# Five edits joined, and the first layer's gradient summed with X and taken through the keys' weight once

## The chip, the cores and the metric

The kernel runs on one core of a Trainium2 chip. A core has TensorE (PE, matmuls into PSUM), VectorE (DVE), ScalarE (ACT), GpSimd (POOL) and SyncE (SP, which only issues transfers here); the compute engines run their own instruction streams and meet at semaphores. The metric is the device time of one execution in microseconds.

## The reference, cut

Four layers follow each other on 4 x 1024 tokens of width 256: gated linear attention, a mixture of 8 experts (2 per token) and a shared one, a test-time memory, and an MLP with ternary weights. Each is added to its input and normalized. The change touches the first and the third. Of the third:

```python
keys = x @ Wk + bk
queries = x @ Wq + bq
values = x @ Wv + bv
alr = MAX_ALR * jax.nn.sigmoid(x @ Wlr + blr).reshape(-1)
def loss_fn(ps):
    pred = _lmm(ps, kf)          # two layers h = h + silu(h @ W + b)
    per_tok = jnp.mean((pred - vf) ** 2, axis=-1)
    return jnp.sum(per_tok * alr)
grads = jax.grad(loss_fn)(params)
new_params = ...                 # p * (1 - LR * WD) - LR * g / (|g| + EPS)
retrieved = _lmm(new_params, queries)
```

The gradient of W1 is keys^T dz1 over all tokens. Since keys = X Wk + bk, it is also Wk^T (X^T dz1) + bk^T (sum of dz1 over the tokens).
Of the first layer: S = gate * S + k v^T per token, y = q S, with 16 heads of 16 and q, k = elu + 1 of projections.

## The kernel before

The kernel is a sequence of blocks of instructions, one stream per engine, with a barrier between blocks. The order inside a stream is the order of the code; no scheduler is involved.

**Attention** (`build_attention`) works on 32 tiles of 128 tokens, tile j being batch j % 4, chunk j // 4. The loop is skewed: step n runs from -5 to 32, and in it each engine takes the scores of tile n + 1, the attention of tile n and the output of n - 1. ScalarE's `project` makes relu(-x), relu(x) and exp of one of four projections (Q = 0 to 3: queries, queries, keys, keys of chunk 0), and `phi` adds two of them, on VectorE for chunk 0 and on GpSimd later. The gates (a sigmoid, 16 heads in each group of 32 rows) go to memory (`gates_out`, four DMAs), and come back spread over all partitions (`gates_in`, 1 MB a tile). `decay(j)` is one scan of 2048 elements on VectorE over them; it gives the decay between all pairs of a tile's tokens. `weigh(j)` multiplies the scores with it, `weigh_k` the transposed keys. SP's queue is the order of all loads: X^T of chunk 0, weights, gates out, gates of tiles 0 and 1, X^T of chunk 1, Wo, and so on.

**Experts** (`build_expert_tiles`): a loop over 71 tiles of gathered rows; its results go to memory (`outs`). Then an own block (`clear_released`, on GpSimd alone) clears semaphores.

**Memory layer** (`build_memory`): 8 blocks of 512 tokens. Before its blocks TensorE zeroes two PSUM banks gW that hold the gradients, and makes the shared expert's last 512 tokens (L1391, L1396). VectorE combines gathered rows (`combine`), takes moments (`scales`), ScalarE normalizes. All other PSUM banks are a ring of three pairs that the uses of a block take in turn (`pair`, 11 uses a block), so a use waits for the reader of the third use before it. TensorE's order in a block q is: second(q), grad1(q-1), turn_h0(q), turn_x(q+1), turn_h1(q), keys, targets, rates of q+1, back(q), turn_dz2(q), first(q+1), grad2(q), turn_dz1(q). `turn_*` are eight transposes each whose results ScalarE copies to the token-major tiles t_h0, t_h1, t_dz2, t_dz1, which are operands of `grad` (L1361). `rates` multiplies X^T with the column Wlr repeated 128 times, so that all 128 partitions hold the same 512 rates; ScalarE's sigmoid makes alr (L1480), and VectorE multiplies with it in `second` (L1638). After block 7 come the last gradient, five `queries` in between, AdamW on VectorE of the biases, W2 and W1 (five operations each), and a barrier. **Read and MLP** (`build_read_and_mlp`) is not touched.

The init semaphore counts VectorE's memsets (1 to 4: ones, zb, bsum, magic) and the two operations that make lr_w (5, 6), which wait for the weights. These lines say who waits there:

```python
pe.wait_ge(init, 6)
for k in range(2):
    pe.matmul(gW[k][:, :], zb[:, 0:P], zb[:, :], start=True, stop=False, skip_group_check=True)
...
v.wait_ge(w_in, 16 * 6)
v.wait_ge(init, 4)
for g in range(G):
    v.tensor_scalar(lr_w[:, g, :], ones[:, :], Wlr[:, g:g + 1], None, ALU.mult).then_inc(init, 1)
```

## Time and profile before

| | |
|---|---|
| median of 3 runs | 1439.4 us (1431.15, 1439.4, 1440.06) |
| the profiled execution | 1432.35 us, span 1430.6 us |
| PE busy in the span | 1333.4 us (93%), 7684 instructions |
| DVE busy | 797.2 us (56%) |
| ACT busy | 577.5 us (40%) |
| POOL busy | 303.3 us (21%) |
| attention | 0 to about 290 us |
| shared expert and routes | to 446 us |
| experts | to 877 us |
| memory layer | 878 to 1193 us |
| read and MLP | 1193 to the end |

TensorE's share is an average over stages. The attention stage has its own limit, the others theirs, and each stage begins when the one before has ended. So each part of the change is read at its own place in the timeline. Times in the rows are from the span's start; "x16" behind a row is the number of instructions merged in it; idle time and its releaser stand in brackets.

### The profile page before, as it was taken

What the parts mean: (1) busy time and instruction counts of PE and PEld (TensorE: products, weight loads), DVE (VectorE), ACT (ScalarE), POOL (GpSimd) and SP (SyncE); (2) the same over time, 40 slices, a digit from 0 to 9 for tenths busy, and PEclk for the clock granted to TensorE, in tenths of its full rate; (3) what the DMA queues carried; (4) which work ended last, traced back from release to release, by engine and by line L of the source; (5) the groups of instructions that cost most, each with busy time, mean ns of one, the idle gap of its engine ahead of it and who ended that gap; (6) DMA issues with size and microseconds to landing.
All of it is one profiled execution on the core that took longest, in us unless ns stands there. A gap on an engine that the chain in (4) does not pass through costs nothing. (4 is left out here: it accounts for less than half of the span.)

```text
span 1430.6 us, 22465 instructions
## 1 busy us (share of the span) xinstructions
PE 1333.4 (93%) x7684; PEld 847.5 (59%) x7685; DVE 797.2 (56%) x1543; ACT 577.5 (40%) x1271; POOL 303.3 (21%) x345
## 2 busy tenths in 40 slices
PE   7999999899998999999999997789999998899995
PEld 4556666655545666666666664345655564577774
DVE  5999999965331222222222221467778656676764
ACT  5577777541101222222222221234444433566665
POOL 2133333314750000000000003522220000244353
PEclk9999999999999999999999998999999999999999
DMA  5665565574220111111111113212110000000001
GB/s 203 207 199 205 206 210 204 198 266 168 99 82 8 37 44 48 47 44 44 44 44 44 48 48 100 78 30 88 30 30 0 1 0 12 1 1 16 30 16 60
DMA packets 76741, 115.83 MB, mean 81 GB/s; under 512 B 10032, under 2 KB 62576, under 8 KB 72560
## 3 DMA queue, kind: packets, MB, share of 16 engines
q1 hardware_dynamic: 70096, 97.89, 20.3%
q0 software_dynamic: 6144, 16.79, 3.6%
q8 instruction: 52, 0.85, 0.2%
q14 instruction: 33, 0.27, 0.1%
q10 hardware_dynamic: 416, 0.03, 0.0%
HBM read 82.86 MB, written 31.82 MB: 80 GB/s over the span
## 5 line engine op out<-in xcount | busy, mean ns | idle before, releaser
L1759 POOL DMA_INDIRECT m_got<-outs,slot x64 | 61.2, 956 | 566.0 <-DMA outs<-XT 453.9
L1164 DVE TENSOR_TENSOR ro_h<-ro_bB,ro_sl 128x512 f32<-128x512 f32 x71 | 49.1, 692 | 217.3 <-PE ro_bB L1113 217.3
L588 DVE TENSOR_TENSOR_SCAN a_dcy<-a_gbc,a_ident 128x2048 f32<-128x2048 f32 x32 | 142.5, 4453 | 6.0 <-DMA a_gbc<-gd 2.2
L2115 POOL TENSOR_TENSOR q_hr<-q_hf,q_hr 128x512 fp32r<-128x512 f32 x64 | 83.9, 1320 | 283.3 <-ACT q_hr L1956 283.3
L1108 PE MATMUL ro_bA<-Win,ro_xT 128*128 x284 | 134.6, 596 | 0.8 <-ACT ro_xT L1135 0.6
L1120 PE MATMUL ro_bO<-Wout,ro_hT 128*128 x568 | 134.3, 379 | 0.9 <-DVE ro_hT L1157 0.9
L1120 PEld LDWEIGHTS ro_bO<-Wout,ro_hT 128*128 128x128 f32 x568 | 107.8, 190 | 45.6 <-issue 34.6
L1113 PE MATMUL ro_bB<-Wsw,ro_xT 128*128 x284 | 133.4, 592 | 0.0
L1144 ACT ACTIVATE XT<-ro_bO 128x256 f32<-128x256 f32 x71 | 27.2, 383 | 204.9 <-PE ro_bO L1120 204.9
L1157 DVE COPY ro_hT<-ro_bH 128x512 f32<-128x512 f32 x71 | 49.1, 691 | 101.2 <-PE ro_bH L1093 101.2
L1113 PEld LDWEIGHTS ro_bB<-Wsw,ro_xT 128*128 128x128 f32 x284 | 54.0, 190 | 67.9 <-issue 67.9
L1881 PE MATMUL q_bO<-W2r,q_hr 128*128 128x256 f32 x512 | 75.8, 293 | 6.8 <-POOL q_hr L2115 6.7
L1139 ACT ACTIVATE ro_sl<-ro_bA 128x512 f32<-128x512 f32 x71 | 42.4, 597 | 96.1 <-PE ro_bA L1108 96.1
L1881 PEld LDWEIGHTS q_bO<-W2r,q_hr 128*128 128x128 f32 x512 | 66.1, 188 | 19.9 <-POOL q_hr L2115 14.2
L597 DVE TENSOR_TENSOR a_A<-a_bS,a_dcy 128x1024 f32<-128x1024 f32 x64 | 75.0, 1212 | 2.3 <-PE a_bS L335 2.3
L1009 POOL DMA_INDIRECT rows<-r_row,r_rix x64 | 63.3, 989 | 61.2 <-DVE r_rix L910 42.1
L676 POOL TENSOR_TENSOR a_qk<-a_eb,a_rb 128x512 f32<-128x512 f32 x28 | 40.0, 1430 | 164.0 <-ACT a_eb L442 164.0
L1871 PE MATMUL q_bH<-q_xr,W1r 128*128 128x512 f32 x256 | 70.7, 404 | 3.6 <-ACT q_hr L1956 3.6
L1108 PEld LDWEIGHTS ro_bA<-Win,ro_xT 128*128 128x128 f32 x284 | 48.3, 190 | 35.5 <-issue 35.2
L1189 PE MATMUL m_ring<-m_h,m_W 128*128 128x512 f32 x128 | 59.9, 612 | 10.0 <-ACT m_alr L1480 6.4
L861 ACT ACTIVATE sh_sl<-sh_bA 128x512 f32<-128x512 f32 x28 | 16.6, 596 | 122.1 <-PE sh_bA L791 67.9
L1955 ACT ACTIVATE q_hf<-q_bH,q_b 128x512 f32<-128x512 f32 x64 | 44.2, 690 | 37.6 <-PE q_bH L1871 36.4
(281 smaller groups left out, 2506.6 us busy)
## 6 DMA issues: line engine op xcount, KB each, us to landing
a_gbc<-gd SPq DMA_DIRECT2D x32, 1024.0 KB, 5.5
rows<-a_zero SPq DMA_DIRECT2D x8, 1152.0 KB, 9.2
XT<-rows SPq DMA_DIRECT2D x71, 128.0 KB, 2.0
outs<-XT SPq DMA_DIRECT2D x71, 128.0 KB, 1.7
a_xt<-in_xTt SPq DMA_DIRECT2D x8, 512.0 KB, 5.8
X<-in_x SPq DMA_DIRECT2D x8, 512.0 KB, 3.9
Win<-in_w_in SPq DMA_DIRECT2D x8, 512.0 KB, 9.8
Wsw<-in_w_sw SPq DMA_DIRECT2D x8, 512.0 KB, 9.8
```

What stands on the lines that cost most here:

```text
L588: v.tensor_tensor_scan(dcy[:, :], gbc[j % 2][:, :], ident16[:, :], 0.0, ALU.mult, ALU.add).then_inc(d_done, 1)
L597: v.tensor_tensor(A[j % 2][:, 2 * h:2 * h + 2, :, :, :].rearrange("p r g e t -> p r g (e t)"), bS[:, 2 * h:2 * h + 2, :].rearrange("p r (g ...
L1009: pool.indirect_dma_start(out=mem["rows"], out_offset=bass.IndirectOffsetOnAxis(ap=rix[p][k][:, 0:1], axis=0), in_=row[p][k][:, :], in_off ...
L1108: mm = pe.matmul(bA[:, :], xT[p][:, g, :], w, start=(g == 0), stop=(g == G - 1))
L1113: mm = pe.matmul(bB[:, :], xT[p][:, g, :], w, start=(g == 0), stop=(g == G - 1))
L1120: mm = pe.matmul(bO[:, 0:D], hT[:, j * P:(j + 1) * P], Wout[:, bass.ds(e, 1), j, :].rearrange("p o f -> p (o f)"), start=(j == 0), stop=(j ...
L1157: v.tensor_copy(hT[:, :], bH[:, :]).then_inc(ht_read, 1)
L1189: mm = pe.matmul(banks[o][:, :], W[:, i, col + o * P:col + (o + 1) * P], rhs(i), start=(i == 0), stop=(i == G - 1))
L1759: pool.indirect_dma_start(out=got[q % 2][k][:, t, :], out_offset=None, in_=mem["outs"], in_offset=bass.IndirectOffsetOnAxis(ap=slot[:, k, ...
L1871: mm = pe.matmul(bH[f % 2][:, :], W1r[:, g, f * P:(f + 1) * P], xr[q % 2][:, part, g, :], start=(g == 0 and part == 0), stop=(g == G - 1 a ...
L1881: mm = pe.matmul(bO[k // 2][:, (k % 2) * D:(k % 2 + 1) * D], hr[:, part, f % 4, k * P:(k + 1) * P], W2r[:, f, :], start=(f == 0 and part = ...
L2115: pool.tensor_tensor(hr[:, 1, f % 4, :], hf[f % 2][:, :], hr[:, 0, f % 4, :], ALU.subtract).then_inc(hl_done, 1)
```

## The change

In attention: `gates_out` and `decays_out` are one DMA each for all 128 rows instead of four, the memory tensors being padded to 32 rows a batch. X^T of chunk 1 is loaded ahead of the first gates. Tile 0's gates come in two halves, and its scan is two scans (`first_decay`), the first behind phi(1), the second behind phi(3). For the keys of chunk 0 ScalarE leaves the relu(x) out, and VectorE takes it from PSUM in one operation with the addition. TensorE has a hand-written step -1.

Between experts and memory layer: the semaphores are cleared by GpSimd inside the experts' block, and an own block for it is gone.

In the memory layer: TensorE's zeroing matmuls wait for 2 memsets instead of 6; ScalarE loads the sigmoid's table before the first normalize; the rates are made for four groups of 128 tokens in 32 columns each, so that 4 rows of a 128 x 128 tile hold all 512, and these go to memory and come back spread over the partitions (two DMAs on SP's queue a block, `spread_rates`); VectorE waits for that load (`al_in`) and no longer for ScalarE. The gradient of W1 is summed as X^T dz1, with the token-major X that is there; turn_h0 and its copies go, and the ring has 10 uses. Behind the last block ScalarE copies the sum (gx), and TensorE takes it through Wk and adds bk times the sums of dz1 (`through_keys`), which `row_of_sums` has turned into a row.

The core of the diff, attention and then the rest:

```diff
-                    for b in range(B):
-                        sp.dma_start(mem["gd"][T, b], gT[T % 2][32 * b:32 * b + H, :]).then_inc(gd_out, 16)
+                    sp.dma_start(mem["gd"][T].rearrange("b h t -> (b h) t"), gT[T % 2][:, :]).then_inc(gd_out, 16)
...
+                        sp.dma_start(gbc[0][:, h * 8 * P:(h + 1) * 8 * P],
+                                     mem["gd"][0, 0, 8 * h:8 * h + 8].rearrange("h t -> (h t)").rearrange("(o n) -> o n", o=1).to_broadcast([P, 8 * P])).then_inc(g0_in[h], 16)
+
+                load_x(1)
                 gates_out(0)
-                gates_in(0)
+                first_gates_in()
                 gates_in(1)
-                load_x(1)
...
+                    if n == -1:
+                        gates(1)
+                        project(4)
+                        turn_k(0)
+                        scores(0)
+                        values(0)
+                        continue
...
-                    act.activation(rb[Q % 2][:, :], projected(Q), ACT.Relu, scale=s).then_inc(qk_read, 1)
+                    if Q != 2 and Q != 3:
+                        act.activation(rb[Q % 2][:, :], projected(Q), ACT.Relu, scale=s).then_inc(qk_read, 1)
                     act.wait_ge(n_done, Q + 1)
-                    act.activation(eb[Q % 2][:, :], nb[:, :], ACT.Exp, scale=-1.0).then_inc(qk_read, 1)
+                    act.activation(eb[Q % 2][:, :], nb[:, :], ACT.Exp, scale=-1.0).then_inc(qk_read, 2 if Q == 2 or Q == 3 else 1)
...
-                    v.tensor_tensor(qk[0][:, Q // 2, Q % 2, :], eb[Q % 2][:, :], rb[Q % 2][:, :], ALU.add).then_inc(phi_done, 1)
+                    if Q < 2:
+                        v.tensor_tensor(qk[0][:, 0, Q, :], eb[Q][:, :], rb[Q][:, :], ALU.add).then_inc(phi_done, 1)
+                    else:
+                        v.scalar_tensor_tensor(out=qk[0][:, 1, Q % 2, :], in0=projected(Q), scalar=0.0, in1=eb[Q % 2][:, :],
+                                               op0=ALU.max, op1=ALU.add).then_inc(phi_done, 1)
...
+                def first_decay(h):
+                    v.wait_ge(g0_in[h], 16)
+                    v.wait_ge(id_done, 1)
+                    c = slice(h * 8 * P, (h + 1) * 8 * P)
+                    v.tensor_tensor_scan(dcy[:, c], gbc[0][:, c], ident16[:, c], 0.0, ALU.mult, ALU.add).then_inc(d_done if h else d0_done, 1)
...
-                    if Q == 1:
-                        decay(0)
+                    if Q == 1 or Q == 3:
+                        first_decay(Q // 2)
```

```diff
+                def spread_rates(q):
+                    sp.wait_ge(lr_read, q + 1)
+                    sp.dma_start(mem["ad"][q], al4[0:P:32, :]).then_inc(al_out, 16)
+                    sp.wait_ge(al_out, 16 * (q + 1))
+                    if q >= 1:
+                        sp.wait_ge(dp_done, 2 * q)
+                    sp.dma_start(alr[:, :], mem["ad"][q].rearrange("k t -> (k t)").rearrange("(o n) -> o n", o=1).to_broadcast([P, 512])).then_inc(al_in, 16)
+
+                for q in range(3):
+                    spread_rates(q)
                 sp.wait_ge(k_read, 2 * 3)
...
                 def keys(q):
                     if q >= 1:
-                        pe.wait_ge(th0_read, 2 * q)
+                        pe.wait_ge(sl2_done, 2 * q)
...
-                    for g in range(G):
-                        mm = pe.matmul(b[0][:, :], lr_w[:, g, :], tokens(q)(g), start=(g == 0), stop=(g == G - 1))
+                    for k in range(4):
+                        for g in range(G):
+                            mm = pe.matmul(b[0][32 * k:32 * k + 32, 0:P], lr_w[:, g, :], XT[:, g, q * 512 + k * P:q * 512 + (k + 1) * P],
+                                           start=(g == 0), stop=(g == G - 1))
...
                 def grad1(q):
-                    pe.wait_ge(th0_read, 2 * (q + 1))
                     pe.wait_ge(td1_read, 2 * (q + 1))
-                    grad(0, "h0", "dz1").then_inc(g1_ready, 1)
+                    grad(0, X[:, 4 * q:4 * q + 4, :], "dz1").then_inc(gx_ready, 1)
+
+                def row_of_sums():
+                    b = pair(NB, Z2)[0]
+                    pe.wait_ge(bsum_done, NB)
+                    for g in range(G):
+                        mm = pe.matmul(b[0:1, g * P:(g + 1) * P], bsum[:, g:g + 1], ident[:, :], start=True, stop=True)
+                    mm.then_inc(sr_ready, 1)
+
+                def through_keys():
+                    pe.wait_ge(gx_read, 1)
+                    pe.wait_ge(sr_read, 1)
+                    pe.wait_ge(bk_in, 16)
+                    for i in range(G):
+                        for j in range(G):
+                            pe.matmul(gW[0][:, i * D:(i + 1) * D], Wk[:, j, i * P:(i + 1) * P], gx[:, j * D:(j + 1) * D], start=(j == 0), stop=False)
+                        mm = pe.matmul(gW[0][:, i * D:(i + 1) * D], bk_row[:, i * P:(i + 1) * P], s_row[:, :], start=False, stop=True)
+                    mm.then_inc(g1_ready, 1)
...
-                pe.wait_ge(init, 6)
+                pe.wait_ge(init, 2)
...
                     second(q)
                     if q >= 1:
                         grad1(q - 1)
-                    turn_h0(q)
                     turn_x(q + 1)
                     turn_h1(q)
...
+                pe.wait_ge(td2_read, 2 * NB)
+                row_of_sums()
                 grad1(q)
...
+                pe.wait_ge(sr_read, 1)
                 queries(3, pair(q + 1, Z2))
+                through_keys()
                 pe.wait_ge(q_read, 2 * 3)
-                queries(4, pair(q + 1, TH0))
+                queries(4, pair(q + 1, TX))
...
-                    act.activation(alr[:, :], pair(q - 1, LR)[0][:, :], ACT.Sigmoid, bias=blr[:, 0:1]).then_inc(lr_read, 1)
+                        act.wait_ge(al_out, 16 * q)
+                    act.activation(al4[:, :], pair(q - 1, LR)[0][:, 0:P], ACT.Sigmoid, bias=blr[:, 0:1]).then_inc(lr_read, 1)
 
...
+                act.wait_ge(init, 4)
+                act.activation(junk[:, :], ones[:, 0:1], ACT.Sigmoid)
                 normalize(0)
...
+                act.wait_ge(sr_ready, 1)
+                act.activation(s_row[:, :], pair(NB, Z2)[0][0:1, 0:D], ACT.Copy).then_inc(sr_read, 1)
+                act.wait_ge(gx_ready, NB)
+                act.activation(gx[:, :], gW[0][:, :], ACT.Copy).then_inc(gx_read, 1)
...
-                    v.wait_ge(lr_read, q + 1)
+                    v.wait_ge(al_in, 16 * (q + 1))
...
-        build_expert_tiles(nc, mem, "ro_", NI, shared=False)
+        build_expert_tiles(nc, mem, "ro_", NI, shared=False, after={"pool": lambda pool: clear_released(nc, pool)})
         experts.close()
-        clear_released(nc)
```

TensorE in attention around step -1, before and then of the change (bS are scores or projections of chunk 0, bQ a projection, bV the values, bK the transposed keys, bY the gates):

```order
L258 MATMUL a_bS<-a_xt0,a_Wqk 128x512 x8
L335 MATMUL a_bS<-a_qm0,a_qk0 128x256 x8
L267 MATMUL a_bY<-a_xt1,a_WgT 32x128 x8
L258 MATMUL a_bQ<-a_xt1,a_Wqk 128x512 x2
L280 MATMUL a_bV<-a_Wv,a_xt0 128x256 x2
L384 MATMUL a_bK<-ident,a_qk0 128x128 x2
L335 MATMUL a_bS<-a_qm1,a_qk0 128x256 x8
```

```order
L263 MATMUL a_bS<-a_xt0,a_Wqk 128x512 x8
L272 MATMUL a_bY<-a_xt1,a_WgT 32x128 x8
L263 MATMUL a_bQ<-a_xt1,a_Wqk 128x512 x2
L389 MATMUL a_bK<-ident,a_qk0 128x128 x2
L340 MATMUL a_bS<-a_qm0,a_qk0 128x256 x8
L285 MATMUL a_bV<-a_Wv,a_xt0 128x256 x2
L340 MATMUL a_bS<-a_qm1,a_qk0 128x256 x8
```

The gates and projection of chunk 1 and the keys' transposes have moved ahead of the first scores, and the values behind them.

VectorE in attention up to the second scan, before and then of the change (a_qk<- is phi, a_dcy<-a_gbc a scan, a_A the weighing, a_kw the weighing of the keys):

```order
L575 MEMSET a_gT 128x1
L579 TENSOR_TENSOR a_qk<-a_eb,a_rb 128x512 x2
L588 SCALAR_TENSOR_TENSOR a_dcy<-a_gbc,a_ident 128x2048
L579 TENSOR_TENSOR a_qk<-a_eb,a_rb 128x512 x2
L597 TENSOR_TENSOR a_A<-a_bS,a_dcy 128x1024 x2
L605 TENSOR_TENSOR a_kw<-a_bK,a_dcy 128x256
L588 SCALAR_TENSOR_TENSOR a_dcy<-a_gbc,a_ident 128x2048
```

```order
L588 MEMSET a_gT 128x1
L593 TENSOR_TENSOR a_qk<-a_eb,a_rb 128x512 x2
L608 SCALAR_TENSOR_TENSOR a_dcy<-a_gbc,a_ident 128x1024
L595 SCALAR_TENSOR_TENSOR a_qk<-a_bS,a_eb 128x512 x2
L608 SCALAR_TENSOR_TENSOR a_dcy<-a_gbc,a_ident 128x1024
L619 TENSOR_TENSOR a_A<-a_bS,a_dcy 128x1024 x2
L627 TENSOR_TENSOR a_kw<-a_bK,a_dcy 128x256
L602 SCALAR_TENSOR_TENSOR a_dcy<-a_gbc,a_ident 128x2048
```

The scan of 2048 in front of two phi has become one of 1024 ahead of them and one behind; these two phi read PSUM.

TensorE in the memory layer, block 1 from second(1) to back(1), before and then of the change (m_ring is the ring of PSUM pairs, m_gW the gradients; the turns of X are written bank by bank in the middle):

```order
L1361 MATMUL m_gW1<-m_t_dz1,m_t_h0 128x256 x8
L1336 MATMUL m_ring00<-ident,m_h0 128x128 x4
L1336 MATMUL m_ring01<-ident,m_h0 128x128 x4
L1292 MATMUL m_ring10<-ident,X 128x128
...
L1336 MATMUL m_ring20<-ident,m_h1 128x128 x4
L1336 MATMUL m_ring21<-ident,m_h1 128x128 x4
L1189 MATMUL m_ring00<-XT,m_Wk 128x512 x2
...
L1311 MATMUL m_ring20<-XT,m_lr_w 128x512 x2
L1189 MATMUL m_ring00<-m_dz2,m_W2T 128x512 x2
```

```order
L1400 MATMUL m_gW1<-m_t_dz1,X 128x256 x8
L1332 MATMUL m_ring20<-ident,X 128x128
L1332 MATMUL m_ring21<-ident,X 128x128
...
L1378 MATMUL m_ring00<-ident,m_h1 128x128 x4
L1378 MATMUL m_ring01<-ident,m_h1 128x128 x4
L1211 MATMUL m_ring10<-XT,m_Wk 128x512 x2
...
L1352 MATMUL m_ring00<-XT,m_lr_w 32x128 x8
L1211 MATMUL m_ring10<-m_dz2,m_W2T 128x512 x2
```

The two groups of h0's transposes are gone, the gradient reads X, and the rates are eight narrow matmuls instead of two wide ones.

## Rows read from the trace of the kernel before

**Rows 1.** Windows, all engines: busy us of each stretch (A:B, its length)
```profile
30.00:60.00 30.00, 25.91 (x321) 16.43 (x320) 29.37 (x27) 16.96 (x44) 8.64 (x5) 0.94 0.61 208
...
1020.00:1050.00 30.00, 29.50 (x113) 18.09 (x112) 22.46 (x54) 12.91 (x23) 6.74 (x8) 1.00 0.11 33
```

**Rows 2.** Timeline, attention's start: start us, us, engine, line, work [idle before]
```profile
10.02 0.82 SPq L205 DMA_DIRECT2D a_gbc<-gd  x2
...
14.66 4.42 DVE L588 TENSOR_TENSOR_SCAN a_dcy<-a_gbc,a_ident 128x2048 f32<-128x2048 f32 x1 [2.16 <-DMA a_gbc<-gd]
...
19.01 1.27 DVE L579 TENSOR_TENSOR a_qk<-a_eb,a_rb 128x512 f32<-128x512 f32 x2
...
22.55 2.35 DVE L597 TENSOR_TENSOR a_A<-a_bS,a_dcy 128x1024 f32<-128x1024 f32 x2 [2.28 <-PE a_bS L335]
...
28.06 4.42 DVE L588 TENSOR_TENSOR_SCAN a_dcy<-a_gbc,a_ident 128x2048 f32<-128x2048 f32 x1
```

**Rows 3.** Timeline, from the experts to the memory layer
```profile
873.37 3.63 SPq L1063 DMA_DIRECT2D outs<-XT  x2
...
878.24 0.39 SPq L1269 DMA_DIRECT2D m_Wk<-in_m_Wk  x1
...
880.32 0.96 POOL L1759 DMA_INDIRECT m_got<-outs,slot  x1 [0.30 <-issue]
...
885.25 1.03 PE L1384 MATMUL m_gW<-m_zb 128*128 128x512 bf16 x2 [9.03 <-DVE m_lr_w L1679]
...
886.08 15.31 PE L1391 MATMUL m_ring<-XT,Ws 128*128 128x512 f32 x32
...
902.77 1.22 DVE L1571 TENSOR_TENSOR X<-X,m_got 128x1024 f32<-128x1024 f32 x1
```

**Rows 4.** Windows, TensorE's granted clock (last but two) before its first matmuls
```profile
884.00:886.00 2.00, 0.75 (x2) 0.47 (x3) 0.48 (x2) 0.00 (x0) 1.62 (x2) 0.50 0.88 307
```

**Rows 5.** Timeline, ScalarE and TensorE at the memory layer's block 0
```profile
925.36 1.26 ACT L1474 ACTIVATE m_vb<-m_ring,m_bias 128x512 f32<-128x512 f32 x2 [6.30 <-remote]
926.65 1.28 ACT L1480 ACT_TABLE_LOAD   x1
928.18 0.69 ACT L1480 ACTIVATE m_alr<-m_ring,m_blr 128x512 f32<-128x512 f32 x1 [0.25 <-remote]
...
929.01 5.80 PE L1189 MATMUL m_ring<-m_h,m_W 128*128 128x512 f32 x8 [6.44 <-ACT m_alr L1480]
...
938.32 3.67 PE L1189 MATMUL m_ring<-m_h,m_W 128*128 128x512 f32 x8 [3.52 <-DVE m_h L1609]
```

**Rows 6.** Timeline, one block of the memory layer, TensorE and VectorE
```profile
1014.31 1.88 PE L1311 MATMUL m_ring<-XT,m_lr_w 128*128 128x512 f32 x4
...
1034.98 1.04 PE L1336 MATMUL m_ring<-ident,m_h 128*128 128x128 f32 x8
...
1038.27 3.67 PE L1189 MATMUL m_ring<-XT,m_Wk 128*128 128x512 f32 x8 [0.50 <-ACT XT L1460]
...
1045.21 1.88 PE L1311 MATMUL m_ring<-XT,m_lr_w 128*128 128x512 f32 x4
1046.93 3.60 PE L1189 MATMUL m_ring<-m_dz,m_W2T 128*128 128x512 f32 x8
...
1034.98 1.29 DVE L1638 SCALAR_TENSOR_TENSOR m_u<-m_u,m_alr 128x512 f32<-128x512 f32 x2
```

**Rows 7.** Timeline, TensorE: the gates in attention, 32 columns wide
```profile
154.43 0.66 PE L267 MATMUL a_bY<-a_xt,a_WgT 128*32 128x128 f32 x16
```

**Rows 8.** Timeline, the end of the memory layer
```profile
1181.49 3.69 PE L1361 MATMUL m_gW<-m_t_dz,m_t_h 128*128 128x256 f32 x16 [1.27 <-ACT m_t_dz L1498]
...
1185.74 0.69 DVE L1738 TENSOR_SCALAR m_ga<-m_gW 128x512 f32<-128x512 f32 x1
...
1191.30 0.69 DVE L1742 SCALAR_TENSOR_TENSOR W1n<-m_W,m_ga 128x512 f32<-128x512 f32 x1
1192.09 1.26 ACT L1519 ACTIVATE XT<-m_ring,m_bq 128x512 f32<-128x512 f32 x2 [2.17 <-PE m_ring L1189]
```

100 lines of the change are left out of this document (49 added, 51 removed).

## The prediction, made before the kernel was run

> **What bounds the kernel now.** I read the stages first. Between 30 and 60 us VectorE is busy 29.37 of 30 us, and between 1020 and 1050 us TensorE is busy 29.50 of 30 us [rows 1]. So the attention loop is bound by VectorE, and the blocks of the memory layer by TensorE. What is taken from VectorE before its loop has begun, or from TensorE inside a block, should therefore come off the end. The timeline then gave the three stretches where an engine waits: the start of attention [rows 2], the change from the experts to the memory layer [rows 3 to 5], and the last block [rows 8].
>
> **Attention's start (-6.5 us).** The gates of tile 0 are asked for at 10.02, and VectorE scans them in one piece from 14.66 to 19.08 [rows 2]. The phi of the keys stands behind that scan, from 19.01 to 20.28, and opens the scores; the weighing follows at 22.55, after 2.28 of waiting for the scores, and the second scan starts only at 28.06. The change splits the first scan, puts a phi on each side, skips two ScalarE activations and takes the first gates in halves. A half of 1 MB: the whole took 4.6 us from its issue (10.02 to 14.66), the floor is nothing, the ceiling 4.6; I take 3.3, as half the bytes leave the fixed part. The gates go out in one issue instead of four, but behind the load of X that now stands ahead of them; that I set at no change but 0.6 us earlier (bounds: 1.7 earlier, 1.4 later). So the first half lands at about 12.8, scan 2.2 us (half of 4.42) to 15.0, phi to 16.4, second half scan to 18.6. The scores can start at 16.5 and be ready by then, so the first weighing starts at 18.7 and takes 2.35. Keys' transposes are now ahead of the scores, so the weighing of the keys no longer waits for them and follows at 21.1 (0.45 us, an estimate from the scan's share of columns: 256 against the weighing's 2048 in 2.35, and a fixed part), the second scan at 21.6 instead of 28.06: 6.5 us. VectorE has no idle behind it, so this reaches the end of the stage. Bounds: 4.5 (gates 2 us late) and 7.5. The merged issues of the later chunks' gates and decays are hidden behind VectorE's full queue; they shorten SP's, and with no cover would gain, not cost.
>
> **Into the memory layer (-9.5 us).** SP's last issue of the experts ends at 877.00 (873.37 + 3.63), its first of the next stage is at 878.24 [rows 3]. Clearing the semaphores inside the experts' block takes away one round of barriers: I take 1.0 of these 1.24 us. TensorE then waits 9.03 us for VectorE's lr_w, which waits for weights; its zeroing matmuls need only two memsets, which are there by 877.9. It starts 7.35 us earlier than 885.25. It had gone to a granted clock of 0.50, the lower level of 1.2 GHz, in that wait [rows 4], and 32 instructions took 15.31 us where 0.43 each, as in the blocks, makes 13.7; with the zeroing 2.1 us more. A wait of 3.52 us ahead of 938.32 did not lower it: eight instructions took 3.67, against 5.80 at 929.01 after 6.44 [rows 5]. The new wait is about 1.8 us, so I count the 2.1 as saved. The shared expert thus ends at 892.1, its product at 892.9, and the first combine, at 902.77 before, starts at 892.9: 9.9. What could hold it back is the gathers of GpSimd, which still begin at 879.0 (the second is at 880.32) as they wait for the experts' rows: one every 1.26 us (0.96 and 0.30 ahead of it) plus some 2 to land has 8 there at 891 and 16 at 901, just when the second combine wants them (9.9 before its time so far, 901). For that I take 0.4 off: 9.5. Bounds: 7.4 (clock at 1.2 GHz all the same), 9.9.
>
> **First rates (-1.6).** ScalarE loads the sigmoid table for 1.28 us directly ahead of the first rates, with TensorE waiting behind them [rows 5]. The change loads it in an idle stretch before the first normalize. The activation shrinks from 512 to 128 columns; of its 0.69 I take 0.3 off (between nothing and all of it). Sum 1.6. ScalarE's 6.30 us wait before 925.36 has a releaser that the profile doesn't name ("remote"). I leave it as it is. TensorE stood 6.44 us ahead of 929.01, of which 1.6 is counted; so if the wait goes, up to 4.8 more is won, and if it grows, that is lost again. The Trainium skill (ScalarE: Activation LUTs, section What ACT_TABLE_LOAD costs) has a switch at about 2.66 us with its drain; by that the saving is 3.0 instead of 1.6. The row speaks against it, as the activations before and after stand only 1.56 us apart.
>
> **The blocks (-14.9).** TensorE per block: the transposes of h0 go, 0.87 us (1.04 with the tail that the next overlaps; eight of 128 columns at a quarter of 0.43), and ScalarE's two copies after them. The rates' four instructions took 1.72 (1045.21 to 1046.93) [rows 6]; they become 16 instructions 32 columns wide, and the attention's gates, the same shape, took 0.66 us [rows 7]. To this I add 0.13 for changing to narrow columns, bounds 0.6 (none) and 1.72 (nothing gained): 0.80, so 0.92 saved. The Trainium skill (TensorEngine Tiling (Array Packing), section Key Properties) says that a change of tiling mode drains the engine, which speaks against this edit, and gives no price; the gates' row bears the drain already, so by the rule too the sum stays within my bounds. The keys wait for X^T, which ScalarE keeps (0.50 idle before 1038.27); with the h0 copies gone it comes 0.13 sooner relative to TensorE. Per block 0.87 + 0.92 + 0.13 = 1.92. VectorE is busy 22.46 of 30 us [rows 1] and still idles some 5 us a block. Block 0 loses only 0.87 + 0.32 + 0.92 = 2.1, because the keys now wait for sl2; blocks 1 to 6 make 11.5, less 0.2 in the block with the ternary scale, where VectorE gets to it 0.2 late; the last block saves 0.87 and the 0.58 for which its queries waited: 1.45. Sum 14.9. The gradient's matmuls with X as weights are the same in number and shape. The new trip of the rates through memory (two DMAs a block on SP's queue) has 18 us: blocks are 30.90 apart (1014.31 to 1045.21), the rates are there at 1016.9 (1014.31 + 1.88 + 0.69) and VectorE uses them at 1034.98 [rows 6]. The broadcast of the gates, four times as large, landed in 4.6 us [rows 2]; two such trips are 9.3 and are covered.
>
> **The end of the layer (+4.1).** The last gradient starts at 1181.49 [rows 8] and takes 3.45; row_of_sums fits into the 1.27 us ahead of it. Behind it queries 3.43, hiding the copy of gx, then through_keys: six matmuls of 256 columns at 0.43, 2.57. So g1 is ready 9.45 after the gradient's start (1190.95), and AdamW of W1 (1185.74 to 1191.99) takes 6.25: end at 1197.4, where ScalarE ended at 1193.35 before. Cost 4.1 in this frame. Uncovered it is at most 3.43 more (if the queries were not in between); below 2.6 it can't fall. TensorE waits some 3.5 us before the next stage, near the 3.52 that did no harm; a lowered clock would cost 2.2.
>
> **Sum**: -6.5 - 9.5 - 1.6 - 14.9 + 4.1 = -28.4. The profiled execution took 1432.35 (span 1430.6), so 1404.0. The median of three is 1439.4; two runs are near 1440, one and the profile near 1431, so a median of the new kernel may sit at 1404 or up to 8 higher. I say 1405.
>
> **Rivals.**
> - *The unexplained ScalarE wait goes* (its instructions and the gathers move): up to 4.8 more, 1399 to 1404. For it: its cause is tied to nothing that must stay. Chance 0.14.
> - *Attention's gain is lost on the way*: the load of X delays the gates by 2 us or more or what TensorE and ScalarE do between the weighings becomes late in place of the scan. Costs 2 to 6.5: 1406 to 1411. For it: the first tiles are the only ones in which VectorE still waits. Chance 0.12.
> - *The blocks give half*: the narrow rates cost 1.72 as before, or the hole of the transposes stays as a wait for X^T. 0.92 times 8 is 7.4: 1412. For it: the 0.50 wait is there already. Against: VectorE and ScalarE have slack. Chance 0.10.
> - *Slower than before: the rates come too late.* One mechanism: SP's trip through memory exceeds 18 us, with the gathers and the 2 MB of ternary weights on the same DMA engines; VectorE then waits in each of 8 blocks. It eats the gain when the trip takes 18 + 28.4/8 = 21.6 us, and is over 1% slower from 23.4. Two landings of 4.6 speak against it. Chance 0.03, then about 1450.
> - *The change does less at the joints*: the clock falls all the same and the barrier stays, +3: 1408. Chance 0.08.
> The forecast itself has 0.53, own range 1400 to 1410.
>
> **Numbers.** The range 1396 to 1414 takes in the first, second, third and last, and the spread of runs of 8 us. Faster by over 1% (what a measurement of this kernel can tell from no change) means under 1425: all cases but the slower one and a pile of losses, 0.91; within 1% 0.06; slower 0.03.
>
> **What would show it.** The second scan at 21.6; TensorE's first matmul of the memory layer at once after the barrier, at a granted clock of 1.00; a table load before the first normalize; blocks 29.0 us apart instead of 30.9, with no wait of VectorE for alr; and DVE's last AdamW 9.4 us behind the last gradient's start and ending the layer. I am wrong if blocks stay over 30 us, if a wait for alr appears, or if the attention's second scan is not 4 us earlier.

## The result, and the profile after

| | before | after |
|---|---|---|
| median | 1438.12 us (20 runs, 1429.54 to 1441.22) | 1430.66 us (20 runs, 1419.56 to 1435.65) |
| ratio to before | | 0.9945, 95% interval [0.9926, 0.9963] |
| profiled execution | span 1430.6, granted clock 0.982 | 1427.51, span 1425.7, granted clock 0.979 |

The forecast was 1405 (1396 to 1414), 28.4 us off the time before. Measured were 7.5 us off. Yet most of the forecast's steps stand in the trace. Line numbers of after: L602 and L608 scans, L1332 transposes of X, L1352 rates, L1378 the other transposes, L1400 gradients, L1439 zeroing, L1446 and L1451 the shared expert's last matmuls, L1516 X^T kept, L1554 transposes kept, L1764 the sums of the shared expert, L1815 gathers.

Attention's start, VectorE in the timeline of after, against [rows 2]: two half scans with the two phi of the keys between them (one merged row of 1.26 us), and the second scan at 22.47 where it was at 28.06.

```profile
13.95 2.29 DVE L608 TENSOR_TENSOR_SCAN a_dcy<-a_gbc,a_ident 128x1024 f32<-128x1024 f32 x1 [1.42 <-DMA a_gbc<-gd]
16.16 1.26 DVE L595 SCALAR_TENSOR_TENSOR a_qk<-a_bS,a_eb 128x512 f32<-128x512 f32 x2
17.34 2.28 DVE L608 TENSOR_TENSOR_SCAN a_dcy<-a_gbc,a_ident 128x1024 f32<-128x1024 f32 x1
19.66 2.36 DVE L619 TENSOR_TENSOR a_A<-a_bS,a_dcy 128x1024 f32<-128x1024 f32 x2
...
22.47 4.42 DVE L602 TENSOR_TENSOR_SCAN a_dcy<-a_gbc,a_ident 128x2048 f32<-128x2048 f32 x1
```

The memory layer in the windows of after, against the second of [rows 1] (columns as there: busy us of PE, PEld, DVE, ACT, POOL, then granted clock, DMA share, GB/s). TensorE is busy 27.26 of 30 us instead of 29.50, with less to do:

```profile
1020.00:1050.00 30.00, 27.26 (x112) 15.88 (x111) 21.22 (x53) 10.59 (x20) 7.75 (x8) 0.98 0.16 44
```

Where it stands is told by the waits of after, ScalarE between 866 and 1190 us (who, what line <- whom: us in total, times, longest). Three rows name nobody of this core (`remote`):

```profile
ACT m_t_dz L1554 <- remote: 22.7, 3, 7.6
...
ACT XT L1516 <- remote: 10.8, 1, 10.8
...
ACT m_al L1536 <- remote: 3.0, 1, 3.0
```

The timeline of after at the earliest of these places, merged rows of three engines:

```profile
885.72 4.70 PE L1451 MATMUL m_ring<-Wout_s,m_dz 128*128 128x256 f32 x21
...
890.70 1.91 PE L1332 MATMUL m_ring<-ident,X 128*128 128x128 f32 x8 [0.29 <-issue]
...
897.94 0.95 POOL L1815 DMA_INDIRECT m_got<-outs,slot  x1 [0.30 <-issue]
902.63 1.29 DVE L1764 TENSOR_TENSOR X<-m_ring,X 128x512 f32<-128x512 f32 x2 [12.62 <-remote]
902.88 1.08 ACT L1516 ACTIVATE XT<-m_ring 128x512 f32<-128x512 f32 x2 [10.76 <-remote]
...
904.11 1.19 PE L1211 MATMUL m_ring<-XT,m_Wk 128*128 128x512 f32 x1 [11.50 <-ACT XT L1516]
```

VectorE waits for L1451, which TensorE had done at 890.4, and ScalarE for L1332, done at 892.6; both go on at 902.6 to 902.9, and TensorE stands 11.50 us for them. Meanwhile GpSimd issued gathers without a break, 24 from 868.68 to 898.9, and the two waits ended 4 us behind the last. The trace also keeps the moments at which semaphores rise (an increment is how an instruction tells the other engines that it is done). The two increments of L1451's matmuls, of which TensorE finished one at 886.96 and the other at 890.41, are there at 902.61 and 902.77, that of L1332 at 902.86. So it was not the work that was late: 3.45 us of matmuls lie between the first two, and 0.16 us between their increments. They had been held up, and came in one burst. From here on such an increment is called late, a run of gathers without a break a train, and the time from one block's rates to the next a step.

The second place comes in three blocks of eight. The timeline of after around 975 us:

```profile
970.49 0.94 POOL L1815 DMA_INDIRECT m_got<-outs,slot  x1 [15.72 <-DVE X L1630]
...
972.25 0.66 PE L1352 MATMUL m_ring<-XT,m_lr_w 128*32 128x128 f32 x16
...
972.85 3.70 PE L1211 MATMUL m_ring<-m_dz,m_W2T 128*128 128x512 f32 x8
...
976.38 1.04 PE L1378 MATMUL m_ring<-ident,m_dz 128*128 128x128 f32 x8
...
979.24 1.08 POOL L1815 DMA_INDIRECT m_got<-outs,slot  x1 [0.30 <-issue]
...
981.92 1.09 ACT L1554 ACTIVATE m_t_dz<-m_ring 128x512 f32<-128x512 f32 x2 [7.56 <-remote]
...
983.15 1.11 PE L1400 MATMUL m_gW<-m_t_dz,m_t_h 128*128 128x256 f32 x4 [2.29 <-ACT m_t_dz L1554]
```

The transposes are done at 977.42, their increment rises at 981.89. From one block's rates to the next it is 29.67, 29.00, 33.21, 31.53, 33.27, 29.00 and 29.38 us: the forecast's 29.0 in two steps, 29.38 in the last (which is 29.38 without any late increment too), 11.0 us too much in the three from 33.21 on; the first takes 23.5 to 25.1 where nothing is late. In each of the three blocks the first late increment is that of the narrow rates themselves: their matmuls end at 972.91, it rises at 973.97. The kernel before had increments late as well, in its shared expert (two waits of ScalarE given to nobody, 25.4 us together) and up to its first values ([rows 5], the 6.30 <-remote), but no such wait in its later blocks.

### The profile page after: what moved, and what is told of

Its sections match the earlier page's. It is cut to its first block and busy times, and to the rows that moved or that the text cites. A ratio compares the mean times of both kernels' runs of the same rounds, so it can differ in the third digit from the quotient of the medians.

```text
span 1425.7 us, 22514 instructions
## 1 busy us (share of the span) xinstructions
PE 1327.9 (93%) x7731; PEld 841.4 (59%) x7733; DVE 795.2 (56%) x1544; ACT 566.7 (40%) x1256; POOL 300.2 (21%) x345
## 5 line engine op out<-in xcount | busy, mean ns | idle before, releaser
L1815 POOL DMA_INDIRECT m_got<-outs,slot x64 | 61.9, 967 | 561.8 <-DMA outs<-XT 447.3
L602 DVE TENSOR_TENSOR_SCAN a_dcy<-a_gbc,a_ident 128x2048 f32<-128x2048 f32 x31 | 138.0, 4453 | 3.9
L1166 ACT ACTIVATE XT<-ro_bO 128x256 f32<-128x256 f32 x71 | 27.2, 383 | 204.9 <-PE ro_bO L1142 204.9
L698 POOL TENSOR_TENSOR a_qk<-a_eb,a_rb 128x512 f32<-128x512 f32 x28 | 36.6, 1306 | 162.8 <-ACT a_eb L455 162.8
## 6 DMA issues: line engine op xcount, KB each, us to landing
Wsw<-in_w_sw SPq DMA_DIRECT2D x8, 512.0 KB, 10.4
```

The costliest lines, as they stand in the source:

```text
L602: v.tensor_tensor_scan(dcy[:, :], gbc[j % 2][:, :], ident16[:, :], 0.0, ALU.mult, ALU.add).then_inc(d_done, 1)
L1815: pool.indirect_dma_start(out=got[q % 2][k][:, t, :], out_offset=None, in_=mem["outs"], in_offset=bass.IndirectOffsetOnAxis(ap=slot[:, k, ...
```

## The experiments

Theories: **D**, the increments are late only while GpSimd's indirect transfers go out; **S** or **M**, they come from the change's own parts or from the layer's work. Within D, **R**: in the blocks what brings them on is the narrow rate matmuls inside a train of gathers; **P**, only where the train lies in the block. And soon **C**: it depends on the chip. The record numbers the chips, but for the one of the first measurement. A chip whose traces show late increments is called late below, one whose traces show none quiet.

**Four runs at once**, all on chip 8. `e1_no_gathers` leaves the experts' outputs out of the sum in X:

```
-  pool.indirect_dma_start(out=got[q % 2][k][:, t, :], ...).then_inc(came[q % 2][k], 16)
+  pool.memset(got[q % 2][k]..., 0.0).then_inc(came[q % 2][k], 64)
```

> The changed kernel without the memory layer's 64 gathers: GpSimd writes small zeros in their place, so the experts' outputs of the second layer's input are left out of the sum in X. Theory G (the new stalls are TensorE's semaphore increments that come late while a train of indirect gathers goes out): every wait that the profile gives to no instruction of the core after 866 us goes (ACT before keep_x 10.8 us, DVE L1764 12.6 us, al4 3.0, three of 7.6 before keep_dz2), all steps from rates to rates are 29.0 us, and the span falls by 11.5 + 3 + 4.2 + 2.5 + 4.3 = 25 us, to about 1400. Rival S (the stalls come from the change's own parts, the early sigmoid, the semaphore clears in the experts' block, the small rate matmuls): they stay, and the span is within 3 us of the changed kernel's 1425.7.

`e2_old_rates` puts the rates back:

```
-  for k in range(4): for g in range(G): mm = pe.matmul(b[0][32*k:32*k+32, 0:P], lr_w[:, g, :], ...)
+  for g in range(G): mm = pe.matmul(b[0][:, :], lr_w[:, g, :], tokens(q)(g), ...)
-  act.activation(al4[:, :], ...)      # and SyncE's two transfers per block
+  act.activation(alr[:, :], ...)
```

> The changed kernel with the rates as before: 4 matmuls of 512 columns, the sigmoid straight into alr, no round trip through memory. Theory R (a block stalls when the narrow rate matmuls run while gathers go out; the three blocks in which they do have the wait of 7.6 us, the one in which they ran just ahead of the gathers has none): the three waits before keep_dz2 go, each step from rates to rates is 29.0 + 1.2 = 30.2 us, rates to rates over all seven 211 to 212 us against 215.05 now, though rates are 1.2 us dearer each; the stall of 11.5 us after the shared expert stays. Rival P (only the place of the gathers in the block matters): three steps stay at 32.5 to 34.5 us, the seven together 220 or more.

`e3_after_rates` and `e4_hold_all` hold gathers back, in fetch(q) of GpSimd:

```
 pool.wait_ge(add2, q - 1)
+pool.wait_ge(lr_read, q - 2)            # e3: for q >= 4 only
+pool.wait_ge(lr_read, max(1, q - 2))    # e4: for q >= 2
```

> The changed kernel, the gathers of block q (q from 4) held back until ScalarE has done the rates of block q-3, about 3.9 us later than now; nothing else. Theory R: the three waits of 7.6 us before keep_dz2 go, the steps are 29.0 us, and the span falls by 11.0 us to about 1415. Rival P2 (it is the transposes of dz2 during a train, whatever the rates do): the transposes are still inside the train, 2 us after its start, and the waits stay, with the steps at 31.5 to 33.3 us.

> As the run before, and the gathers of blocks 2 and 3 also wait until ScalarE has done the first rates, so that only 16 gathers go out at the layer's start and not 24. Theory G: TensorE's increments of the shared expert's last matmuls and of the first transposes come when the 16 gathers are done, about 890 us, and the stall of 11.5 us shrinks to at most 2: the first keys' start at about 894 against 904.1, and the span at about 1405. Rival L: 16 gathers from about 905 us on hold the increments of the first block as they did in the kernel before (6.4 us at its first matmuls), and 4 to 8 us of the gain are given back: span 1409 to 1413. Rival S: the first stall stays, span 1415.

Measured, one run each: 1389.4, 1402.6, 1386.4 and 1395.9 us, with 1418.3 for the kernel before. None of the four had a single wait given to nobody, not even in the routes stage, where nothing had been edited. Neither theory had foreseen that: this was a quiet chip, with no late increments to remove. What the four do tell is the price of a block: steps of 29.00 us with the change and 29.92 with the old rates, where the kernel before has 30.90 ([rows 6], and on chip 5 below). So the rates give 0.92 us a block and the gradient 0.98.

**The pair itself, again.** The two kernels unedited on one chip (chip 5), and the holds beside them:

> The changed kernel, nothing edited, beside the kernel before on one chip. In the four runs ahead of this, on another chip than the first profiles, no late increment of TensorE was seen at all, also where nothing had been done against it. Theory C (the late increments during gathers belong to the chip or its moment, and cost the changed kernel more than the one before): if no wait of this profile is given to no instruction of the core, the changed kernel is 28 to 32 us faster than the one before (ratio about 0.979), rates to rates is 29.0 us in every block and the first keys come about 12 us earlier than in the first profile. If the waits are there again, the ratio is 0.992 to 0.997 as in the first measurement. Rival (the four runs were quiet because each had an edit that removes the cause): the waits are there, with the ratio near 0.9945, on any chip.

> The kernel before, nothing edited. Theory C: on a chip where the changed kernel shows no such waits this one shows none either (in the first profile it had 25.4 us of them in the shared expert and 13.8 us around the first keys), its attention ends and its experts end where they did to within 2 us plus what the shared expert gains, and the span is 1412 to 1420. Rival: it shows them as in the first profile, and the span is about 1430.

> The changed kernel with the gathers from block 4 on held back until the rates are done, again, now beside the unedited one. Theory C on a quiet chip: the same as the unedited kernel to within 2 us, since there is nothing for the hold to remove. On a chip with the late increments: the three waits of 7.6 us before keep_dz2 go if the narrow rate matmuls inside a train bring them on (11 us faster than the unedited one), and stay if any train over the transposes does.

Measured: after 1388.58 us (1387.85 to 1391.99), before 1418.78 (1416.95 to 1422.51), ratio 0.9789 [0.9765, 0.9814]; the hold 0.9815 [0.9794, 0.9837]; e4's kernel once more, 1395.4. C holds on this chip, and its rival is out: the unedited kernels have no late increment. The expectation for the old kernel here (1412 to 1420) met 1416.8. The hold changed nothing in the steps of 29.00, and its runs were 5 us slower; its profile has TensorE at the lower level at other places, and for 39 us in all against 25 of the unedited one's. That this alone makes the 5 us is not shown. Timeline of the unedited changed kernel on this chip, TensorE from the experts' end to the first rates:

```profile
864.30 0.60 PE L1439 MATMUL m_gW<-m_zb 128*128 128x512 bf16 x2 [1.78 <-DVE m_magic L1731]
864.74 13.90 PE L1446 MATMUL m_ring<-XT,Ws 128*128 128x512 f32 x32
879.49 7.17 PE L1451 MATMUL m_ring<-Wout_s,m_dz 128*128 128x256 f32 x32 [0.85 <-DVE m_dz L1758]
886.96 1.91 PE L1332 MATMUL m_ring<-ident,X 128*128 128x128 f32 x8 [0.29 <-ACT X L1510]
890.14 3.67 PE L1211 MATMUL m_ring<-XT,m_Wk 128*128 128x512 f32 x8 [1.27 <-ACT XT L1516]
...
897.17 0.66 PE L1352 MATMUL m_ring<-XT,m_lr_w 128*32 128x128 f32 x16
```

and of the kernel before on it:

```profile
875.81 1.03 PE L1384 MATMUL m_gW<-m_zb 128*128 128x512 bf16 x2 [8.99 <-DVE m_lr_w L1679]
876.64 15.15 PE L1391 MATMUL m_ring<-XT,Ws 128*128 128x512 f32 x32
892.64 7.17 PE L1396 MATMUL m_ring<-Wout_s,m_dz 128*128 128x256 f32 x32 [0.85 <-DVE m_dz L1702]
...
903.48 5.14 PE L1189 MATMUL m_ring<-XT,m_Wk 128*128 128x512 f32 x8 [1.27 <-ACT XT L1460]
```

32 gathers went out in one train there (864.9 to 906.2), longer than the 24 of the first profile, and with the narrow rates inside it; the keys still started 1.27 us behind the transposes. Train, rates and their round trip through memory alone make nothing late on such a chip. A third quiet one, chip 7, was the same (e1's kernel 1389.1, e4's 1387.1, the kernel before 1419.9).

**A chip with late increments.** The next two runs met one (chip 14, the kernel before: 1435.05). `u1_start_undone` undoes the layer's start, `s1_more_landings` adds loads:

```
 u1:  -  pe.wait_ge(init, 2)                +  pe.wait_ge(init, 6)
      -  after={"pool": clear_released}     +  a block of its own for it
 s1:  +  for k in range(48):
      +      sp.dma_start(extra[:, 4*k:4*k+4], io["m_Wk"][0:P, 4*k:4*k+4]).then_inc(extra_in, 16)
```

> The changed kernel with the layer's start as before: TensorE waits for the rates' weight columns ahead of its first matmul, and the semaphores are cleared in a block of their own. By the prediction's term (TensorE starts 7.0 us earlier and the gather queue 1.6 us earlier) this costs 6 to 10 us: the zero matmuls 8 to 9.5 us behind SyncE's last store of the experts against 1.3 to 1.6 us in the changed kernel, the first keys 6 to 8 us later, and the span 1392 to 1397 on a quiet chip. Rival (the layer's start waits for the gathers, the earlier TensorE gains nothing): under 2 us. If the chip has late increments in the scatters, the first keys' stall is shorter than 11.5 us, since TensorE's last matmuls come nearer the end of the gathers.

> The changed kernel with 48 small loads more on SyncE (128 rows of 16 bytes into a spare tile) between the layer's weights and the first rates' round trip, about 870 to 895 us, inside the first gathers, so that landings raise semaphores about three times as often there. Theory Q (increments of TensorE are late where the semaphores are raised too often for the chip): waits given to no instruction of the core come up in 870 to 900 us, the first keys start 2 us or more later than in the unedited kernel (890.1), and records of landings are missing there. Rival: nothing of it on a quiet chip, the first keys within 1 us and only the first block longer, by up to 5 us, if the round trip of the rates comes late behind the loads.

u1 took 1428.46 us, s1 1424.65. In u1 the zero matmuls start 7.7 us behind SyncE's last store (870.44 to 878.17), and 1.6 in the changed kernel's first profile (866.72 to 868.27): 6.2 of the 6 to 10 expected. But the first keys come 37.1 us behind that store, against 37.4 with the start changed. In the first profile of the kernel before it was 37.1 too (876.67 to 913.74), and on chip 5 it fell from 36.2 to 27.2. On a late chip the earlier start is worth nothing up to the first keys, as long as the train behind it is 24 long (n3 below has 16); the late increments take it back whole. s1 was meant for a quiet chip and decides nothing about Q. Its first keys came 37.9 us behind the store, half a microsecond more than in the first profile, though its shared expert was held up and its first combine came 6 us later. Both had the three waits before L1554, of 7.46 to 7.51 us.

**The deciding three**, on one more chip of that kind (chip 3, the kernel before: 1437.84), with kernels e4, e2 and e1 again, one run each:

> The changed kernel with the gathers held back (blocks 2 and 3 until the first rates, from block 4 on until the rates of block q-3). Wanted on a chip with late increments in the scatters. Theory R (in the blocks they come up when the narrow rate matmuls run inside a train): no wait of 7.5 us before keep_dz2, all steps after the first 29.0 us; and the first keys start at about 30 us behind SyncE's last store of the experts (37.4 in the first profile), since only 16 gathers go out at the start. Rival P2 (any train over the transposes of dz2): three waits of 7.5 us stay. On a quiet chip: span 1385 to 1396, nothing decided.

> The changed kernel with the rates as before (4 matmuls of 512 columns, sigmoid straight into alr). On a chip with late increments theory R expects no wait of 7.5 us before keep_dz2 and steps of 29.9 us, with the gathers lying over the rates as they do now; rival P (the place of the train in the block, which the other two parts of the change moved) expects three waits and steps of 32 to 34 us. On a quiet chip as before: steps 29.92.

> The changed kernel without the memory layer's gathers (the experts' outputs are left out of the sum in X). On a chip with late increments in the scatters theory D (only GpSimd's indirect transfers bring them on) expects no wait given to no instruction of the core after 866 us, 29.0 us in every block and a span 25 to 35 us shorter than the first profile's 1425.7; rival M (the memory layer's own work does) expects them to stay. On a quiet chip: span about 1388.

n1, without gathers: 1395.81 us. Its waits in the routes stage (ScalarE, 300 to 448 us), which still has its scatters, show the kind of chip, and its layer, in the timeline, has nothing late:

```profile
ACT sh_sl L883 <- remote: 15.9, 2, 10.0
```

```profile
884.49 7.17 PE L1451 MATMUL m_ring<-Wout_s,m_dz 128*128 128x256 f32 x32 [0.86 <-DVE m_dz L1758]
891.95 1.91 PE L1332 MATMUL m_ring<-ident,X 128*128 128x128 f32 x8 [0.29 <-ACT X L1510]
895.13 3.67 PE L1211 MATMUL m_ring<-XT,m_Wk 128*128 128x512 f32 x8 [1.27 <-ACT XT L1516]
```

The first keys are 27.2 us behind the last store (867.96), as on a quiet chip, and the steps between the first and the last are 29.00. D stands, M and S are out. What of the gathers does it (their issue, their bytes or their landings) is not separated.

n2, old rates: 1419.89 us. All of its steps are 29.92 but the first and the last (30.15), while the gathers lie over the rates just as in after (timeline of n2):

```profile
971.50 1.88 PE L1347 MATMUL m_ring<-XT,m_lr_w 128*128 128x512 f32 x4
...
976.65 1.04 PE L1372 MATMUL m_ring<-ident,m_dz 128*128 128x128 f32 x8
...
977.73 1.09 ACT L1548 ACTIVATE m_t_dz<-m_ring 128x512 f32<-128x512 f32 x2 [3.62 <-PE m_ring L1372]
```

ScalarE takes the transposes at once, 6.8 us into a train that began at 969.8, and the wide rates' increment rises 0.02 us behind their end. P is out. The edit takes the rates' round trip through memory away too, so it doesn't tell the narrow matmuls from the trip. The stall after the shared expert stays (11.9 us of VectorE), as expected.

n3, gathers behind the rates: 1407.16 us, 30.7 less than the kernel before on that chip. The rates end at 967.1, the train begins at 968.81, and ScalarE takes the transposes at once (timeline of n3):

```profile
966.41 0.66 PE L1352 MATMUL m_ring<-XT,m_lr_w 128*32 128x128 f32 x16
...
968.81 0.94 POOL L1816 DMA_INDIRECT m_got<-outs,slot  x1 [20.60 <-ACT m_al L1536]
...
970.54 1.04 PE L1378 MATMUL m_ring<-ident,m_dz 128*128 128x128 f32 x8
...
971.61 1.08 ACT L1554 ACTIVATE m_t_dz<-m_ring 128x512 f32<-128x512 f32 x2 [3.57 <-issue]
...
978.30 1.04 PE L1378 MATMUL m_ring<-ident,m_dz 128*128 128x128 f32 x8
...
980.72 1.09 ACT L1554 ACTIVATE m_t_dz<-m_ring 128x512 f32<-128x512 f32 x2 [2.45 <-PE m_ring L1378]
```

Two increments are late all the same, at the train's end: that of the gradient (L1400) is due at 978.46 and rises at 980.60, that of the next transposes is due at 979.34 and rises at 980.70. It is so in all three blocks (2.0 to 2.1 us and 1.2 to 1.4), and the steps stay 29.00 all the same.

Over after, u1, s1 and n3: of nine blocks with the narrow rates inside a train of eight all have the wait of 7.5 us, of six with them just ahead of one (after, u1 and s1 one each, n3 three) none. R stands for this wait, with the round trip as a part of it that no run takes out alone. In n3 the trip is issued at the train's start (968.06 and 969.66, the train from 968.81), in after 4 to 5.5 us into it (974.39 and 975.97); so it does no harm at the start, and further in it is untested. For the narrow matmuls speaks that their own increment is 1.0 to 1.1 us late in all nine blocks, before SyncE has issued the trip. The first keys came 27.8 us behind the store, better than the 30 expected. Against that, there is one new wait in block 0, in the train of the 16 gathers of blocks 2 and 3 (910.3 to 930.1), and no narrow rates run inside it. So a train of 16 makes increments late without them. With TensorE at the lower level behind the wait, the second step took 32.02 us, where 29.0 were expected:

```profile
933.25 1.09 ACT L1554 ACTIVATE m_t_h<-m_ring 128x512 f32<-128x512 f32 x2 [8.82 <-remote]
```

**The version drawn from this**, `v1_hold_each`: behind the first 16 gathers every train 8 long and right behind the rates, beside the unedited kernel and the same hold in the kernel before.

```
 pool.wait_ge(add2, q - 1)
+pool.wait_ge(lr_read, q - 1)    # for q >= 2
```

> The changed kernel with the gathers of block q (q from 2) held back until the rates of block q-2 are done, so that they go out in trains of 8 right behind the rates, with time to land before the sum of block q wants them (13 us behind a train of 10). Theory D with R: on a chip with late increments the stall of 8.8 us that the last hold still had in block 0 (a train of 16) goes too, all steps after the first 29.0 us, and the ratio to the kernel before is 0.970 to 0.978; no wait of 7.5 us. On a quiet chip: the same as the unedited changed kernel to within 5 us (whose clock dips differ), ratio 0.979 to 0.983. Rival: a hold as late as this makes the sums in X wait for the gathers, and the steps grow to 30 us or more on either chip.

> The changed kernel, nothing edited, on the same chip. If the scatters show late increments: as the first measurement, ratio 0.990 to 0.997, three waits of about 7.5 us before keep_dz2 and one of 10 to 12 us before keep_x. If not: ratio 0.977 to 0.982.

> The kernel before with the same hold. It has no narrow rates, and its blocks had no such wait, so on a chip with late increments only its first keys can gain: the 6.3 us before its first values, and the first steps (31.64 and 31.08 against 30.90), in all 5 to 9 us of the 1430.6, so that the changed kernel's hold is worth more than the old one's by 15 us or more. On a quiet chip: nothing, within 2 us of 1416.8.

The chip (11) was a quiet one: 1389.98 us, ratio 0.9800 [0.9784, 0.9817], for v1; 1391.90, ratio 0.9808 [0.9791, 0.9825], unedited; 1420.99 for the old kernel with the hold (one run), against 1418.17 without (1417.94 to 1423.93), a little over the 2 us that were allowed for. So the hold costs the changed kernel nothing there, its steps are 29.00, and what it gives on a chip with late increments is measured only in its sister n3. That v1 has no wait of 8.8 us there is argued, not shown.

What the semaphore records say over these runs, by stage: landings (the increments by which a transfer tells that it has arrived) recorded of those due, then TensorE's increments that rose over 0.9 us behind the end of their matmul, and the latest of them. On the late chips some of TensorE's own increments have no record either, 4 to 10 of some 70 in the layer, and the others are matched in order; so the counts are good to a few, and the 17 us of the routes are rough. The largest that hangs on no matching is the 15.7 us in n2's layer.

```
                   chip    routes and shared expert      experts              memory layer to 1060 us
before             first    864 of 1328, 20, 17.1 us    2223 of 2224, none    374 of 1232,  7,  8.6 us
after              first    772 of 1296, 20, 17.2       2208 of 2224, none    445 of 1408, 17, 15.6
u1_start_undone    14       832 of 1296, 16, 17.5       2224 of 2224, none    478 of 1408, 20,  9.5
n1_no_gathers      3        766 of 1280, 21, 17.2       2208 of 2224, none    352 of  416, none
n2_old_rates       3        756 of 1296, 22, 17.2       2208 of 2224, none    339 of 1248,  7, 15.7
b0_before_again    5       1440 of 1344, none           2223 of 2224, none   1233 of 1232, none
a0_after_again     5       1375 of 1280, none           2208 of 2224, none   1367 of 1440, none
```

(A few landings fall across a stage's border.) On the first chip, 14 and 3 landings leave no record of their own where the scatters and gathers run, 35 to 42% of them in the routes and 66 to 73% in the layer, and there alone increments are late; on 5, 7, 8 and 11 no increment is.

## Why the prediction was right and wrong

The steps, measured on chip 5 where both kernels ran undisturbed (place in the trace before, after, difference), beside the sum's terms:

| up to | before | after | gained in this stretch | forecast |
|---|---|---|---|---|
| last scan of attention ends | 284.14 | 278.29 | 5.85 | 6.5 |
| SyncE's last store | 867.27 | 862.97 | -1.55 | 0 |
| first combine | 892.50 | 879.35 | 8.85 | 9.5 |
| first matmul on h (m_h, m_W) | 915.51 | 898.95 | 3.41 | 1.6, and 0.9 of the blocks' |
| last rates | 1124.03 | 1095.02 | 12.45 | 14.9 less 0.9 and the last block's 1.45 |
| next stage's first matmul | 1179.55 | 1153.06 | -2.52 | -4.1 and the last block's 1.45 |
| end | 1416.79 | 1386.07 | 4.23 | 0 |

The five stretches that the sum had priced gave 28.0, against 28.4: it was right where the increments are on time. That all together make 30.7 is the two stretches at nothing, -1.55 and 4.23.

**Attention**: the mechanism as forecast, the first half 1.15 us late (13.95 against 12.8, though its issue went out about as early as assumed, at 9.57), the second scan 0.9 (22.47 against 21.6): half the bytes did not land in the 3.3 us assumed, they took 4.4, where the whole had taken 4.6.

**Into the memory layer**: TensorE starts at once, at full clock, and its 32 matmuls take 13.90 against 15.15. Right on a quiet chip, 8.85 of 9.5. In the first profile the first combine came 19.7 us earlier as well (883.10 against 902.77 [rows 3]; 9.95 of that came with the earlier end of the experts), and 10.2 us of it were lost at the next step.

**First rates**: the table load gave less than forecast. Of the 3.41 us of the stretch 1.5 are the first keys at full clock (5.14 to 3.67) and 1.2 the narrow matmuls. More than half of the 1.6 was there already: on chip 5 the table load of the kernel before runs while TensorE does the rates (913.38 to 914.66, the rates end at 913.78), so TensorE's wait only fell from 1.73 to 1.11. The 1.6 had been read at a place that a late increment had stretched: in [rows 5] the load is over at 927.93 and ScalarE still waits, 0.25 us <-remote, so there the load was not what TensorE waited for.

**The blocks**: 30.90 to 29.00 in the five steps between the first and the last, 1.90 against the 1.92 worked out; 31.13 to 29.38 in the last. No wait for alr in any run; the rival of rates that come too late is out, and so is that of blocks that give half. The narrow matmuls cost 0.66 us and 0.92 was saved, with no room for a dearer change of shape than the 0.13 counted.

**The end**: VectorE starts the last AdamW 10.4 us behind the last gradient's start (1135.83 to 1146.26), 9.45 forecast; the two rows of biases take 0.6 us each and had not been counted. The forecast's own sum had a slip of 0.2 (1190.95 and 6.25 are 1197.2, not 1197.4). 2.5 against 2.65 for the stretch.

**The end of the run** was 4.2 shorter, unforeseen. With 1.55 lost ahead of the layer, both are stretches whose work is the same; what differs in them is when TensorE's clock is at its lower level: 17 us of the last stretch before, 8 after.

**The step that failed** is the sentence on ScalarE's 6.30 us: "I leave it as it is." The wait with a releaser that the profile doesn't name was there, in [rows 5], and I took it for something that stays, goes (4.8 more won) or grows (that much lost again), all at that one place. It was a sign of a disturbance that can act where TensorE hands something on while gathers go out; ScalarE's 25.4 us <-remote in the shared expert, which the forecast never mentions, was another. The change moves two things into that: the first combine frees its buffers so early that 24 gathers go out in one train instead of 16, and three hand-overs inside it come late, and the rates become narrow and fall inside the trains. Spans of the first chip less chip 5: 13.8 us for the kernel before, 39.7 for the changed one. Of the 13.8, 9.4 lie ahead of the layer and 4.7 between the store and the last rates. Of the 39.7, 10.2 lie between SyncE's last store and the first keys, 8.6 from there to the second rates (waits, and TensorE at its lower level behind them), 11.0 in the three blocks, 3.8 ahead of the layer, and 6.1 behind it. The difference of 25.9 is what the gain lacks in the profiled executions; it would be 31.5 had the changed kernel not also lost 5.65 us less than the old one ahead of the layer, which no term of the forecast held. That gathers are behind the stall and the three blocks is shown by taking them away (n1) and by moving them (n3), one run each on chip 3; the waits they are compared with stand in the first profile and, on chip 14, in u1 and s1; the 6.1 behind the layer have no late increment in them, only a lower clock. None of my rivals held it, and the range, drawn from rows of one chip with the run's spread of 8 us, could not.

What stays open: why some chips hold increments back and others not, why the narrow matmuls (or their round trip deep in the train, which no run tells from them) bring the long wait on in a train of eight when wide ones don't, and what in the gathers does it. It isn't the chip's speed: from the experts' first matmul to SyncE's last store the changed kernel takes 418.8 us in the first profile and 420.5 on chip 5.

## What to carry to other kernels

A wait whose releaser the profile can't name is not a constant. Compare the end of the matmul that it waits for with the wait's end, look for what other engine is busy throughout, and price every hand-over that the change would move into that stretch. And keep trains of indirect transfers short, behind the matmuls whose results are wanted: one added wait on GpSimd's queue (v1) cost nothing on a quiet chip, and on a late chip the gain with a like hold (n3) stood at 30.7 us where the first measurement had 7.5. That 30.7 is one run against one, and the unedited changed kernel was not run on that chip; in the first measurement the runs of one kernel spread over 12 to 16 us. Take the measurement on more than one chip before a change is judged by it: the same pair gave 0.9945 and 0.979.

## What was not expected of the hardware

- On two of the six numbered chips, and on the first, TensorE's increments rose up to 15.7 us behind their matmuls' end while GpSimd's indirect transfers went out or just behind them, several within 0.2 us of each other; in the experts between, without such transfers, none was over 0.9 us late in any of the runs of the table.
- The same program's TensorE clock falls to its lower level (1.2 GHz) at places that shift from chip to chip, and one kernel (e3's) had a span of 1384.6 us on one quiet chip and 1394.0 on another, with the same steps of 29.00 in its blocks: no edit is behind the difference. A wait of 3.52 us, which in [rows 5] was followed by eight matmuls in 3.67 us, was followed by eight in 5.07 in the changed kernel on chip 5 (906.14), so that row alone does not tell what a wait does to the clock.
- Landings raise the semaphore in sixteen steps: for the layer's 64 gathers 1015 of 1024 increments are recorded on chip 5. The Trainium skill (DMA: Bandwidth & Descriptors, section Why a DMA increments its semaphore by 16 and not by 1) says so, and the trace agrees. On the first chip 272 of them are.
